# Attention, then a top-8 lookup: the masked logits and their extreme in one VectorE instruction

## The chip, the cores and the metric

One core of one Trainium2 chip runs the whole program. The metric is the device time of one execution in microseconds. The kernel before took 624.84 us, the median of 3 runs (624.62 to 629.85).

## The reference, cut to what matters

16 batches of 128 rows by 1024 columns go through a cross attention and then through a feed-forward part with a table of 256 slots. The change touches the second part alone:

```python
query = hidden_states @ Wq.T
rq = query @ Wr.T
rk = aux_keys @ Wr.T
router_scores = einsum(rq, rk) / sqrt(48) + log_rel
top_scores, top_idx = top_k(router_scores, 8)
sel_keys = aux_keys[top_idx]
attn = einsum(query, sel_keys) / sqrt(64) + log_rel[top_idx]
w = softmax(attn)
aux_out = (w @ aux_values[top_idx]) @ Wvd.T @ Wvu.T
out = hidden_states + gate * aux_out
```

For each of the 128 rows of a batch, the 8 best of 256 router scores choose which 8 slots take part in a softmax over other scores, the key products.

## The kernel before, in words

The five engines run programs of their own that are written out by hand and tied together by semaphores. There is no planner: the order of the calls in each engine's block is the order of the work.

**Main part.** The attention and the hidden layer of the feed-forward part take the first 572 us or so. Nothing of it is changed but one weight preparation: `scoreB`, a matrix of 65 used rows by 512 columns. Columns 0 to 255 give router scores, columns 256 to 511 key products, and row 64 (`BOT`) holds `log_rel`, brought by two DMAs from POOL's queue (L1143). ScalarE scales the key half at L978 and the router half at L982, in the second period of the attention.

**Tail.** From L757 (TensorE), L1020 (ScalarE), L1191 (GpSimd) and L1486 (VectorE) on, 16 batches pass through a pipeline. Batch b goes through these steps:

- TensorE: `score` (L617) makes 512 columns in PSUM, router scores and key products side by side.
- VectorE: `top_max` (L1337) finds the best eight, `top_replace` (L1342) writes a copy of the scores in SBUF with those eight replaced by `NEG` = -3e38, `top_mask` (L1347) compares that copy with the scores in PSUM: 1 where nothing was replaced. `top_logits` (L1353) adds NEG times that mask to the key products, `logit_max` (L1358) takes the negated maximum.
- ScalarE: `softmax_exp` (L1001) with the sum of the row, then copies for TensorE.
- TensorE: `w_transpose` (L726), `z_product` (L734), and with VectorE's `z_low` (L1368, the low part of the product) `f_product` (L748, L749).
- For batches 0 to 11 ScalarE scales the result (`f_scale`, L1018), GpSimd adds the hidden state (L1196, both inputs in SBUF) and SP stores it. `output_scale` (L1180) on GpSimd gives the scale of two batches at a time from `weight_reciprocal` (L1364) and the gate. For batches 12 to 15 VectorE does both in `finish` (L1377).

VectorE's order for step i is: `top_replace(i)`, `z_low(i-3)`, `top_mask(i)`, `top_max(i+1)`, `top_logits(i)`, at even i `weight_reciprocal`, `logit_max(i)`. In step 2 the last two `query_copy` (L1300) stand behind `top_replace(2)`; TensorE passes L754 only when they are done. The steps for batches 0 and 1 are part of VectorE's `hidden_step(15)` and `hidden_step(16)`. In steps 2 and 3 the gate is worked out (`gate_argument`, `gate_value`).

TensorE's order for step i is: `score(i+1)`, `z_product(i-2)`, `w_transpose(i-1)`, `f_product(i-3)`.

Of the kernel before, what the change touches and what calls it, by code (L numbers as in the profile page):

```python
# [6 lines left out]
ALU = mybir.AluOpType  # L7
ACT = mybir.ActivationFunctionType
AX = mybir.AxisListType.X
# [24 lines left out]
BOT, RDIM, NSLOT, TOPK, VB = 64, 48, 256, 8, 64  # L34
UH = N // 4
UQ = UH + BOT
NEG = -3.0e38
# [3 lines left out]
def wait(engine, sem, value):  # L41

    if value > 0:
        engine.wait_ge(sem, value)
# [12 lines left out]
def attention_ffn_kernel(nc, x, ctx_rows, ctx_cols, WqT_raw, WkT_raw, Wv_rows, WoT_rows, bo_row, g_col, Wuq_cols,  # L57
# [3 lines left out]
    with ctx:  # L61
        def sb(name, shape, dt=F32, scope=ctx):
            return scope.enter_context(nc.sbuf_tensor(name, shape, dt))

        def sem(name):
            return ctx.enter_context(nc.semaphore(name))
# [11 lines left out]
        scoreB = sb("scoreB", [P, 2 * NSLOT])  # L78
# [93 lines left out]
        replaced = sb("replaced", [P, NSLOT], scope=ffn)  # L172
        outside = sb("outside", [P, NSLOT], scope=ffn)
        logits = sb("logits", [P, 2, NSLOT], scope=ffn)
        nlmax = sb("nlmax", [P, 2], scope=ffn)
        w_sb = sb("w_sb", [P, 2, NSLOT], scope=ffn)
# [38 lines left out]
        def score_psum(b):  # L215

            return k_slot[:, b * HALF:(b + 1) * HALF] if b < 2 else small[b % 2]
# [4 lines left out]
        def queries(b):  # L222

            if b == B:
                return range(B - 2, B)
            return range(2 * (b - EARLY - 1), 2 * (b - EARLY))
# [15 lines left out]
        log_rel_in = sem("log_rel_in")  # L242
# [18 lines left out]
        b1_prod = sem("b1_prod")  # L261
        score_ready = sem("score_ready")
        score_zeros = sem("score_zeros")

        x_stats = sem("x_stats")
        x_mv = sem("x_mv")
# [85 lines left out]
        masked = sem("masked")  # L352
        outside_done = sem("outside_done")
        logits_ready = sem("logits_ready")
# [117 lines left out]
        def _(pe):  # L472
# [113 lines left out]
            def h_transpose(b, k):  # L586
                pe.wait_ge(h_done, b + 1)
                wait(pe, hT_hi_done, b - 1)
                wait(pe, hT_lo_done, b - 1)
                for j in range(J):  # L590
                    last = nc.tensor.transpose(slot[k][:, j * P:(j + 1) * P], hbuf[:, k, j * P:(j + 1) * P],
                                               ident[:, :])
                last.then_inc(h_T, 1)

            def hidden_products(b, k):
                pe.wait_ge(hT_hi_done, b + 1)
                pe.wait_ge(hT_lo_done, b + 1)
                before = b if b < EARLY else b - 1
                wait(pe, units_biased, before)
                wait(pe, rows_copied, before)  # L600
                dst = unit_psum(b)
                for j in range(J):
                    for n, (a, c) in enumerate(((0, 0), (1, 0), (0, 1))):
                        last = nc.tensor.matmul(dst[:, 0:UQ], hT[a][:, k, j, :], WuqT[c][:, j, :],  # L604
                                                start=(j == 0 and n == 0), stop=(j == J - 1 and n == 2))
                last.then_inc(units_prod, 1)
# [12 lines left out]
            def hidden_step(b):  # L619
                if b + 1 < B:  # L620
                    if b == 0:
                        pe.wait_ge(q_sub, 4 * B)
                    h_transpose(b + 1, (b + 1) % 2)
                if b == EARLY + 5:
                    pe.wait_ge(logsum_done, 1)
                    pe.wait_ge(query_done, 2 * (b - EARLY - 1))
                    nc.tensor.matmul(logtotal_psum, ones[:, :], logsum[:, :], start=True, stop=True).then_inc(logtotal, 1)
                if b < B:
                    if b == 0:
                        pe.wait_ge(mt_copied, B)  # L630
                        pe.wait_ge(wuq_hi, 1)
                        pe.wait_ge(wuq_lo, 1)
                    if b == EARLY:
                        pe.wait_ge(x1_done, B)
                    if b < B - 1:
                        hidden_products(b, b % 2)
                if b > EARLY:
                    if b == EARLY + 1:
                        pe.wait_ge(units_biased, EARLY)
                        pe.wait_ge(o_copied, 2 * B)  # L640
                        pe.wait_ge(query_ones, 1)
                    if b == EARLY + 5:
                        pe.wait_ge(normv_step, 1)
                    for n in queries(b):
                        query_transpose(n, n % 2)
                if b == B - 2:
                    pe.wait_ge(log_rel_in, 16 * 2)
                    for n in range(2):
                        score(n)
                if b == B - 1:  # L650
                    hidden_products(b, b % 2)
                    pe.wait_ge(query_done, B - 2)
                    for n in range(2, 4):
                        score(n)
# [83 lines left out]
            def f_product(b, k):  # L738
                pe.wait_ge(z_split, b + 1)
                if b == 0:  # L740
                    pe.wait_ge(logits_ready, 2)
                if b - 2 < B - BY_VECTOR:
                    wait(pe, f_scaled, b - 1)
                else:
                    pe.wait_ge(y_last, b - 2 - (B - BY_VECTOR) + 1)
                for n in range(2):
                    cols = slice(n * HALF, (n + 1) * HALF)
                    nc.tensor.matmul(slot[k][:, cols], zT[:, k, :], WvuT_hi[:, cols], start=True, stop=False)  # L748
                    last = nc.tensor.matmul(slot[k][:, cols], zT[:, k, :], WvuT_lo[:, cols], start=False, stop=True)  # L749
                last.then_inc(f_prod, 1)  # L750
# [17 lines left out]
        def _(act):  # L768
# [150 lines left out]
            for b in range(PERIODS):  # L919
                p, o, e = b - 1, b - 2, b - 3  # L920
                for i in range(4):
# [48 lines left out]
                    if b == 1 and i == 1:  # L970
                        act.wait_ge(vv_prod, NSLOT // P)
                        act.wait_ge(rk_prod, 1)
                        nc.scalar.copy(VV[:, :, :].rearrange("p s (r d) -> p s r d", d=VB),
                                       ob[:, 0:2 * VB].rearrange("p (s d) -> p s d", d=VB).unsqueeze(2).broadcast_to(
                                           [P, NSLOT // P, P // VB, VB])).then_inc(vv_copied, 1)
                        nc.scalar.copy(rkT, ob[0:RDIM, NSLOT:2 * NSLOT]).then_inc(rk_copied, 1)
                        act.wait_ge(score_zeros, 1)
                        nc.scalar.mul(scoreB[0:BOT, NSLOT:2 * NSLOT], keysT,  # L978
                                      float(BOT) ** -0.5).then_inc(score_ready, 1)
                    if b == 1 and i == 3:  # L980
                        act.wait_ge(b1_prod, 1)
                        nc.scalar.mul(scoreB[0:BOT, 0:NSLOT], ob[0:BOT, 0:NSLOT],  # L982
                                      float(RDIM) ** -0.5).then_inc(score_ready, 1)
# [12 lines left out]
                hidden_step(b)  # L996

            def softmax_exp(b, k):
                act.wait_ge(logits_ready, b + 1)
                wait(act, w_T, b - 1)  # L1000
                nc.scalar.activation(w_sb[:, k, :], logits[:, k, :], ACT.Exp, bias=nlmax[:, k:k + 1],  # L1001
                                     accum_out=wsum[:, b, :]).then_inc(w_done, 1)

            def wT_copy(b, k):
# [15 lines left out]
            for i in range(1, B + 2):  # L1020
                if has(i - 1):
                    softmax_exp(i - 1, (i - 1) % 2)
                if i == 1:
# [4 lines left out]
                                         scale=0.5).then_inc(gate_tanh, 1)  # L1028
                if i == 3:
                    act.wait_ge(gate_arg, 1)  # L1030
                    nc.scalar.activation(gb[:, :], ga[:, :], ACT.Tanh, bias=half3[:, 2:3],
                                         scale=half3[:, 1:2]).then_inc(gate_tanh, 1)
# [168 lines left out]
        def _(dve):  # L1201
            V = nc.vector
# [141 lines left out]
            def top_mask(b):  # L1344
                dve.wait_ge(top_step, 2 * b + 2)
                wait(dve, masked, b)
                V.tensor_tensor(outside[:, :], replaced[:, :], score_psum(b)[:, 0:NSLOT],  # L1347
                                ALU.is_equal).then_inc(outside_done, 1)

            def top_logits(b):  # L1350
                dve.wait_ge(outside_done, b + 1)
                wait(dve, w_done, b - 1)
                V.scalar_tensor_tensor(logits[:, b % 2, :], outside[:, :], NEG, score_psum(b)[:, NSLOT:2 * NSLOT],  # L1353
                                       ALU.mult, ALU.add).then_inc(masked, 1)

            def logit_max(b):
                dve.wait_ge(masked, b + 1)
                V.tensor_reduce(nlmax[:, b % 2:b % 2 + 1], logits[:, b % 2, :], AX, ALU.max,  # L1358
                                negate=True).then_inc(logits_ready, 1)

            def weight_reciprocal(b):

# [206 lines left out]
```

## Time and profile before

| | |
|---|---|
| median of 3 runs | 624.84 us |
| the profiled execution | 622.58 us |
| its span | 620.8 us |
| PE busy | 592.5 us, 95% of the span |
| DVE busy | 541.1 us, 87% |
| ACT busy | 418.1 us, 67% |
| POOL busy | 409.7 us, 66% |

Of the profiled execution's 622.58 us, 620.8 are the span that the trace covers; 1.8 us lie around it. PE is TensorE (PEld its weight loads), DVE is VectorE, ACT ScalarE, POOL GpSimd. A share of busy time is a mean over parts with different limits; here the tail, the last 49 us, is the part that counts. Starts are microseconds from the span's beginning. Consecutive VectorE instructions overlap a little in the trace, so what one costs the engine is the step from its start to the next start.

### The profile page before, as it was taken

What the parts mean: (1) busy time and instruction counts of PE and PEld (TensorE: products, weight loads), DVE (VectorE), ACT (ScalarE), POOL (GpSimd) and SP (SyncE); (2) the same over time, 40 slices, a digit from 0 to 9 for tenths busy, and PEclk for the clock granted to TensorE, in tenths of its full rate; (3) what the DMA queues carried; (4) which work ended last, traced back from release to release, by engine and by line L of the source; (5) the groups of instructions that cost most, each with busy time, mean ns of one, the idle gap of its engine ahead of it and who ended that gap; (6) DMA issues with size and microseconds to landing.
All of it is one profiled execution on the core that took longest, in us unless ns stands there. A gap on an engine that the chain in (4) does not pass through costs nothing.

```text
span 620.8 us, 11452 instructions
## 1 busy us (share of the span) xinstructions
PE 592.5 (95%) x3718; PEld 516.5 (83%) x3718; DVE 541.1 (87%) x721; ACT 418.1 (67%) x864; POOL 409.7 (66%) x421
## 2 busy tenths in 40 slices
PE   4999999999999999999999999999989799999896
PEld 3778888888888888888888888888878799998574
DVE  5999999999999999999999999999968544866996
ACT  5566667676777676767676676777666576584783
POOL 4964457787767768687878787767655735430494
PEclk9999999999999999999999999999999899999999
DMA  8849695868687685959595868676563600000156
GB/s 315 223 128 231 189 248 167 216 180 207 188 201 212 171 231 154 243 173 242 162 243 169 219 179 204 197 195 175 134 196 109 180 8 2 2 2 0 59 214 271
DMA packets 63530, 106.11 MB, mean 171 GB/s; under 512 B 11392, under 2 KB 43680, under 8 KB 61168
## 3 DMA queue, kind: packets, MB, share of 16 engines
q1 hardware_dynamic: 52576, 84.32, 46.4%
q10 hardware_dynamic: 10000, 18.62, 13.2%
q0 software_dynamic: 896, 2.45, 1.3%
q8 instruction: 30, 0.49, 0.4%
q14 instruction: 28, 0.23, 0.1%
HBM read 46.62 MB, written 25.17 MB: 116 GB/s over the span
## 4 chain that ended last, share of the span: by engine, by line
PE 83%; DVE 4%; DMA 3%; ACT 3%; issue 3%; POOL 2%; ACTq 1%; DVEq 0%; SPq 0%; POOLq 0%
PE ob L548 18%; PE gm L517 16%; PE gm L604 5%; PE q_slot L475 4%; PE turn L501 4%; PE k_slot L477 4%; PE k_slot L475 4%; PE q_slot L477 4%; PE k_slot L476 4%; PE q_slot L476 4%; PE turn L604 4%; PE gm L526 2%; PE turn L559 2%; DMA Wuq_in<-Wuq_cols 2%; PE turn L734 1%
## 5 line engine op out<-in xcount | busy, mean ns | idle before, releaser
L1067 POOL TENSOR_TENSOR qs_sb<-qs_sb,qrec 128x1024 f32<-128x1024 f32 x64 | 122.0, 1906 | 96.3 <-DVE qrec L1257 96.1
L548 PEld LDWEIGHTS ob<-mt_sb,q_hd 128*128 128x128 f32 x1024 | 124.3, 194 | 8.3 <-ACT q_hd L805 3.0
L548 PE MATMUL ob<-mt_sb,q_hd 128*128 128x128 f32 x1024 | 127.9, 279 | 2.4 <-ACT q_hd L805 2.4
L517 PE MATMUL gm<-ekT,ctxT 128*128 128x256 f32 x512 | 118.2, 379 | 0.0
L517 PEld LDWEIGHTS gm<-ekT,ctxT 128*128 128x128 f32 x512 | 95.9, 190 | 13.6
L800 ACT ACTIVATE qs_sb<-qs_sb 128x1024 f32<-128x1024 f32 x64 | 67.9, 1061 | 47.3 <-DVE qs_sb L1246 45.9
L790 ACT ACTIVATE ek<-k_slot,nkm 128x1024 f32<-128x1024 f32 x62 | 69.1, 1114 | 32.7 <-DVE nkm L1221 32.5
L1221 DVE TENSOR_REDUCE nkm<-k_slot 128x1 f32<-128x1024 f32 x62 | 74.0, 1194 | 13.9 <-PE k_slot L477 13.9
L1253 DVE TENSOR_REDUCE qsum<-qs_sb 128x16 f32<-128x1024 f32 x64 | 77.1, 1205 | 7.6 <-ACT qs_sb L800 6.5
L1246 DVE TENSOR_TENSOR qs_sb<-q_slot,qm 128x1024 f32<-128x1024 f32 x64 | 78.4, 1224 | 2.2
L1228 DVE STREAM_TRANSPOSE kt<-ek 128x1024 f32<-128x1024 f32 x64 | 79.0, 1234 | 1.1 <-DMA ekT<-kt 1.1
L1240 DVE TENSOR_REDUCE qm<-q_slot 128x16 f32<-128x1024 f32 x64 | 76.0, 1187 | 0.5 <-issue 0.5
L475 PE MATMUL k_slot<-ctx_hi,WkT_hi 128*128 128x512 f32 x124 | 54.7, 441 | 9.3 <-DVE ctx_lo L1419 7.1
L475 PE MATMUL q_slot<-WqT_hi,xn_hi 128*128 128x512 f32 x128 | 53.0, 414 | 2.3 <-DVE qs_sb L1246 2.3
L1061 POOL TENSOR_TENSOR xn_lo<-xn,xn_hi 128x1024 fp32r<-128x1024 f32 x16 | 38.3, 2396 | 20.2 <-ACT xn_hi L784 20.2
L477 PE MATMUL q_slot<-WqT_lo,xn_hi 128*128 128x512 f32 x128 | 50.3, 393 | 0.0
L476 PE MATMUL q_slot<-WqT_hi,xn_lo 128*128 128x512 f32 x128 | 50.0, 391 | 0.0
L477 PE MATMUL k_slot<-ctx_lo,WkT_hi 128*128 128x512 f32 x124 | 49.3, 398 | 0.0
L476 PE MATMUL k_slot<-ctx_hi,WkT_lo 128*128 128x512 f32 x124 | 49.1, 396 | 0.0
L796 ACT COPY g_sb<-gm 128x512 f32<-128x512 f32 x16 | 9.4, 587 | 54.6 <-PE gm L517 54.6
L845 ACT ACTIVATE junk<-o_sb 128x128 f32<-128x128 f32 x128 | 37.6, 297 | 4.8 <-issue 4.7
L1266 DVE STREAM_TRANSPOSE qt<-qs_sb 128x1024 f32<-128x1024 f32 x32 | 38.0, 1188 | 0.0
(208 smaller groups left out, 1309.9 us busy)
## 6 DMA issues: line engine op xcount, KB each, us to landing
ekT<-kt SPq DMA_DIRECT2D x488, 64.0 KB, 2.9
q_turned<-qt SPq DMA_DIRECT2D x16, 1024.0 KB, 4.8
q_hd<-q_turned ACTq DMA_DIRECT2D x64, 256.0 KB, 5.7
ctx_in<-ctx_rows SPq DMA_DIRECT2D x16, 512.0 KB, 6.1
x_all<-x SPq DMA_DIRECT2D x16, 512.0 KB, 4.7
ctxT<-ctx_cols SPq DMA_DIRECT2D x16, 512.0 KB, 5.5
out<-q_hd SPq DMA_DIRECT2D x15, 512.0 KB, 2.6
Wuq_in<-Wuq_cols ACTq DMA_DIRECT2D x1, 1280.0 KB, 9.3
```

The source lines that it names most:

```text
L475: nc.tensor.matmul(dst, lhs[0], rhs[0], start=True, stop=False)
L476: nc.tensor.matmul(dst, lhs[1], rhs[0], start=False, stop=False)
L477: return nc.tensor.matmul(dst, lhs[0], rhs[1], start=False, stop=True)
L517: last = nc.tensor.matmul(gm[:, cols], ctxT[:, b % 2, j, :], ekT[:, 2 * half:2 * half + 2, :, j * BLK:(j + 1) * BLK], start=(j == 0), stop ...
L548: last = nc.tensor.matmul(ob[:, (j % 4) * C:(j % 4 + 1) * C], q, mt_sb[:, b % 2, t, :], start=(t == 0), stop=(t == T - 1))
L790: nc.scalar.activation(ek[:, i % 2, :], k_psum(b, i)[:, :], ACT.Exp, bias=nkm[:, i:i + 1], accum_out=ksum[:, b % 2, i:i + 1]).then_inc(k_e ...
L1067: nc.gpsimd.tensor_tensor(e, e, qrec[:, i % 2, :].unsqueeze(2).broadcast_to([P, PAIR, DH]), ALU.mult).then_inc(q_mul, 1)
L1221: V.tensor_reduce(nkm[:, i:i + 1], k_psum(b, i)[:, :], AX, ALU.max, negate=True).then_inc(k_max, 1)
L1228: V.transpose(kt[:, i, :], ek[:, i % 2, :]).then_inc(k_T, 1)
L1240: V.tensor_reduce(qm[:, :], q, AX, ALU.max).then_inc(q_max, 1)
L1246: V.tensor_tensor(qs_sb[:, i % 2, :].rearrange("p (m d) -> p m d", d=DH), q, qm[:, :].unsqueeze(2).broadcast_to([P, PAIR, DH]), ALU.subtra ...
L1253: V.tensor_reduce(qsum[:, :], qs_sb[:, i % 2, :].rearrange("p (m d) -> p m d", d=DH), AX, ALU.add).then_inc(q_sum, 1)
```

## The change

The key products and `log_rel` beside them are negated, so that the extreme wanted is a minimum. `top_mask` no longer compares with PSUM: it looks for the constant NEG in the replaced copy and multiplies by 3e38 in the same instruction, a `tensor_scalar` from SBUF to SBUF. `top_logits` becomes a `tensor_tensor_reduce` that adds and keeps the minimum, and `logit_max` has no instruction left. ScalarE's exponential takes the scale -1. One ScalarE instruction on one row of 256 is added in the attention's second period, behind a wait for the two DMAs of `log_rel`. Who waited for `logits_ready` now waits for `masked`.

```diff
@@ TensorE, hidden_step
                 if b == B - 2:
                     pe.wait_ge(log_rel_in, 16 * 2)
+                    pe.wait_ge(log_turned, 1)
@@ TensorE, f_product
-                    pe.wait_ge(logits_ready, 2)
+                    pe.wait_ge(masked, 2)
@@ ScalarE, second period
                         nc.scalar.mul(scoreB[0:BOT, NSLOT:2 * NSLOT], keysT,
-                                      float(BOT) ** -0.5).then_inc(score_ready, 1)
+                                      -float(BOT) ** -0.5).then_inc(score_ready, 1)
                     if b == 1 and i == 3:
+                        act.wait_ge(log_rel_in, 16 * 2)
+                        nc.scalar.mul(scoreB[BOT:BOT + 1, NSLOT:2 * NSLOT], scoreB[BOT:BOT + 1, NSLOT:2 * NSLOT],
+                                      -1.0).then_inc(log_turned, 1)
@@ ScalarE, softmax_exp
-                act.wait_ge(logits_ready, b + 1)
+                act.wait_ge(masked, b + 1)
                 wait(act, w_T, b - 1)
-                nc.scalar.activation(w_sb[:, k, :], logits[:, k, :], ACT.Exp, bias=nlmax[:, k:k + 1],
+                nc.scalar.activation(w_sb[:, k, :], logits[:, k, :], ACT.Exp, bias=nlmax[:, k:k + 1], scale=-1.0,
@@ VectorE, top_mask
-                V.tensor_tensor(outside[:, :], replaced[:, :], score_psum(b)[:, 0:NSLOT],
-                                ALU.is_equal).then_inc(outside_done, 1)
+                V.tensor_scalar(outside[:, :], replaced[:, :], NEG, -NEG, ALU.not_equal, ALU.mult).then_inc(outside_done, 1)
@@ VectorE, top_logits and logit_max
-                V.scalar_tensor_tensor(logits[:, b % 2, :], outside[:, :], NEG, score_psum(b)[:, NSLOT:2 * NSLOT],
-                                       ALU.mult, ALU.add).then_inc(masked, 1)
+                V.tensor_tensor_reduce(logits[:, b % 2, :], outside[:, :], score_psum(b)[:, NSLOT:2 * NSLOT], 1.0, -NEG,
+                                       ALU.add, ALU.min, nlmax[:, b % 2:b % 2 + 1]).then_inc(masked, 1)
 
             def logit_max(b):
-                dve.wait_ge(masked, b + 1)
-                V.tensor_reduce(nlmax[:, b % 2:b % 2 + 1], logits[:, b % 2, :], AX, ALU.max,
-                                negate=True).then_inc(logits_ready, 1)
+                pass
```

## Rows read from the trace of the kernel before

**Rows 1.** Busy time by engine in 22 us of the tail
```profile
583.00:605.00 22.00, 22.00 (x109) 16.12 (x108) 20.66 (x68) 19.70 (x46) 21.69 (x14) 1.00 0.47 192
```

The columns: the stretch and its length, then busy us of PE, PEld, DVE, ACT and POOL with the number of instructions, the granted clock, the DMA share, GB/s.

**Rows 2.** Chain that ended last, one step of the tail: start, us, what
```profile
586.29 0.86 PE ob L617 x2
...
588.75 0.86 PE gm L617 x2
```

**Rows 3.** PE's timeline: start, us, instruction, idle before and its releaser
```profile
576.02 0.41 PE L726 MATMUL turn<-ident,w_sb 128*128 128x128 f32 x2 [2.25 <-issue]
...
579.43 0.68 PE L734 MATMUL turn<-wT,VV 128*128 128x128 f32 x4 [0.74 <-DVE zT L1368]
...
608.88 0.68 PE L734 MATMUL turn<-wT,VV 128*128 128x128 f32 x4 [0.53 <-DVE zT L1368]
```

**Rows 4.** DVE's timeline at the head of the tail
```profile
573.98 0.41 DVE L1358 TENSOR_REDUCE nlmax<-logits 128x1 f32<-128x256 f32 x1
...
575.18 0.48 DVE L1300 COPY query<-q_slot 128x128 f32<-128x128 f32 x2
```

**Rows 5.** DVE's timeline, one step of the tail
```profile
595.66 0.08 DVE L1342 MATCH_VALUE_LOAD replaced<-top,gm 128x8 f32 x1
...
596.50 0.42 DVE L1347 TENSOR_TENSOR outside<-replaced,gm 128x256 f32<-128x256 f32 x1
597.00 0.43 DVE L1337 MAX8 top<-ob 128x8 f32<-128x256 f32 x1
...
597.78 0.42 DVE L1358 TENSOR_REDUCE nlmax<-logits 128x1 f32<-128x256 f32 x1
598.12 0.08 DVE L1342 MATCH_VALUE_LOAD replaced<-top,ob 128x8 f32 x1
```

**Rows 6.** POOL's timeline, first and last pair of its twelve adds
```profile
583.29 4.72 POOL L1196 TENSOR_TENSOR q_hd<-q_hd,x_all 128x1024 f32<-128x1024 f32 x2
...
607.86 4.73 POOL L1196 TENSOR_TENSOR q_hd<-q_hd,x_all 128x1024 f32<-128x1024 f32 x2
```

**Rows 7.** ACT's timeline: the first scaling of a result
```profile
581.52 1.11 ACT L1018 ACTIVATE q_hd<-k_slot,oscale 128x1024 f32<-128x1024 f32 x1
```

**Rows 8.** One line each: count, duration ns min/median/max, first and last start
```profile
L1457 DVE TENSOR_SCALAR bo_bc<-bo_bc x1: 186/186/186, 19.4 to 19.4; 128x128 f32<-128x128 f32 x1
...
L1116 POOL TENSOR_SCALAR x_all<-x_all,one_rstd,nb x16: 1194/1206/1638, 485.0 to 560.4; 128x1024 f32<-128x1024 f32 x16
```

**Rows 9.** DVE and POOL side by side, timeline from 539 to 544 us
```profile
539.16 1.23 DVE L1479 CAST WvuT_hi<-WvuT_in 128x1024 fp32r<-128x1024 f32 x1
...
539.83 1.64 POOL L1116 TENSOR_SCALAR x_all<-x_all,one_rstd,nb 128x1024 f32<-128x1024 f32 x1
...
541.43 2.38 POOL L1187 TENSOR_TENSOR WvuT_lo<-WvuT_in,WvuT_hi 128x1024 fp32r<-128x1024 f32 x1
541.44 2.65 DVE L1304 TENSOR_TENSOR units<-units,Wu 128x256 f32<-128x256 f32 x1
543.79 1.38 POOL L1116 TENSOR_SCALAR x_all<-x_all,one_rstd,nb 128x1024 f32<-128x1024 f32 x1
```

**Rows 10.** Timeline at the end of the tail, last mask and last exponential
```profile
608.77 0.42 DVE L1347 TENSOR_TENSOR outside<-replaced,ob 128x256 f32<-128x256 f32 x1
...
610.13 0.51 ACT L1001 ACTIVATE w_sb<-logits,nlmax 128x256 f32<-128x256 f32 x1
```

**Rows 11.** The two DMAs of log_rel: duration of the issue, first and last start
```profile
L1143 POOL DMA_DIRECT2D scoreB<-log_rel_row x2: 509/512/516, 27.1 to 27.6; - x2
```

**Rows 12.** Timelines of ACT and POOL where the new ACT instruction goes
```profile
43.81 1.11 ACT L870 ACTIVATE mt_sb<-gm,krec 128x128 f32<-128x128 f32 x4
...
45.77 0.46 POOL L1073 TENSOR_TENSOR mt_sb<-mt_sb,bo_bc 128x128 f32<-128x128 f32 x1
```

**Rows 13.** Groups by line in the tail: busy us, mean ns, idle before
```profile
L1001 ACT ACTIVATION_READ_ACCUMULATOR w_sb<-logits,nlmax 128x1 f32 x16 | 3.0, 187 | 0.0
...
L1001 ACT ACT_TABLE_LOAD x1 | 1.3, 1283 | 0.0
```

More of the change, by code:

```diff
@@ L263, in attention_ffn_kernel @@
         score_zeros = sem("score_zeros")
+        log_turned = sem("log_turned")
         x_stats = sem("x_stats")
```

## The prediction

> **What bounds the kernel now.** All the edits but one lie in the tail, so I read the tail. First the busy time by engine of a stretch in its middle: TensorE works 22.00 of 22.00 us, GpSimd 21.69, VectorE 20.66 [rows 1]. Then the chain of waits, which runs through TensorE there: a score product starts at 586.29 and the next at 588.75, so a step takes 2.46 us, all of it TensorE's own work [rows 2]. Shortening VectorE's part of such a step gives nothing. GpSimd has the same rate by its own length: twelve adds, in pairs from 583.29 to 607.86 for the first and last, which is 24.57 us for ten batches or 2.457 us each [rows 6]. Then TensorE's timeline at both ends, where it does wait: until 576.02 for the two query copies, 0.74 us for the low part of the first z, 0.53 us for one near the end [rows 3]. VectorE sets these. So the reduction that goes away can pay at the head and at the end, not in the eleven steps between.
>
> **The change part by part, if VectorE and GpSimd leave each other alone.** One reduction costs VectorE 0.34 us (597.78 to 598.12) [rows 5]. The mask now takes 0.42 us [rows 5]. The new one is a one-source instruction from SBUF to SBUF; the only such row of size has half the elements and takes 0.186 us [rows 8]. Bounds 0.19 and 0.42; I take 0.25, near the row of its own kind, a gain of 0.17. The fused add-and-minimum shows nowhere. The nearest rows are the mask and the reduction, 0.42 us each over the same 256 elements; above them I put ScalarE's separate reading of a sum, 0.187 us more, and as the far bound its table load, 1.283 us more [rows 13]. No row excludes that it is a little shorter than the two-operand instruction it replaces, so the low bound is 0.40. I take 0.42, since it reads and writes what its neighbours do.
>
> Head: reduction 1 (573.98) stands before the query copies (575.18) [rows 4], and so does mask 1. TensorE starts 0.34 + 0.17 = 0.51 us sooner. Reduction 2 stands before the gate's arithmetic and the first `z_low`, on which TensorE waits at 579.43 [rows 3]: 0.34 more, of which the trace's overlaps leave about 0.3. TensorE is then about 0.8 us ahead and busy without a gap. Reduction 3 and mask 3 also precede the gate and the second reciprocal, so GpSimd's first add comes about 1.05 us sooner, at 582.24.
>
> End: the `z_low` before the wait at 608.88 stands behind reduction 14, so 0.34 us more. The last exponential (610.13) waited for reduction 15 [rows 10]; it moves by the same 0.34, not twice, because the copy in front of it comes from TensorE. Sum: 0.8 + 0.34 = 1.15 us gained.
>
> ScalarE's added instruction costs nothing. Its DMAs were issued by 27.6 us plus 0.5 [rows 11], sixteen microseconds before the place. It pushes `mt_scale` (43.81, 1.11 us) by about 0.4 us, and who waits is GpSimd's bias add, which started at 45.77 [rows 12] behind a longer instruction of its own queue: 44.92 + 0.4 is 45.3, still earlier. If that cover were gone it would cost 0.4 us once. The added waits on TensorE name work finished long before; 0 to 0.05 us each. The other renamed waits come with the same instruction as before or an earlier one.
>
> **The part that speaks against it.** The new mask may need what GpSimd holds. At 541.43 GpSimd starts an add-like instruction with two SBUF inputs, 2.38 us; VectorE starts a two-input one at 541.44 whose row says 2.65 us, where the same 256 elements otherwise take 0.42. It ends 0.28 us after GpSimd's: it stood still for the whole of it. The GpSimd instruction behind it took 1.38 us instead of 1.206 [rows 8, 9]. A one-source instruction from SBUF did it too: during VectorE's cast at 539.16 (1.23 us), GpSimd's took 1.64, 0.43 more than its median. The old mask read one operand from PSUM and ran at 0.42 us while GpSimd was adding [rows 5]. The new one is of the cast's kind, and GpSimd adds almost without a pause from 583 to 612.6.
>
> The Trainium skill says so outright: in "SBUF — State Buffer", section "Who interferes with whom", a VectorE `tensor_scalar` in a mode that uses both its ports and a GpSimd instruction exclude each other, and the later one stands still until the first is done. By that page this mask stands still; by the rate of 0.186 us alone the sum would stay at a gain of 1.15 us. The measured stall of [rows 9] agrees with it for other operations.
>
> What it costs: VectorE's step without waits is 2.46 less the reduction 0.34, less the faster mask 0.17, less the 0.16 us in which `top_max` waited for TensorE (597.00 against 596.50 + 0.34) [rows 5], about 1.8 us. So each mask from batch 5 on arrives during an add and waits some 0.6 us for its end, and VectorE falls into step with GpSimd: one mask between two adds. That alone would be free but for two things. First, an add waits for the mask in its way: by [rows 8, 9] 0.17 us behind 256 two-input elements and 0.43 behind 1024 one-source elements; for 256 one-source ones I take 0.04 to 0.17. Second, the chain from a mask to the next add: mask 0.25, `top_max` 0.35, fused instruction 0.42, exponential 0.51 [rows 10], scaling 1.11 [rows 7] and the signals between come to 2.7 us, against an add of 2.36. With one add a step the two balance at 2.5 to 2.6. So a step costs 2.50 to 2.61 us, I take 2.55.
>
> The last mask, batch 15, comes after eleven adds: 582.24 + 11 x 2.55 = 610.3, against 608.77 [rows 10]. Behind it the reduction is gone, so the last exponential starts 0.74 us later, 611.0 against 610.13: 0.9 us later, and the final additions and stores follow it. With 2.50 it is 0.4 us, with 2.61 1.6 us. Forecast: +0.9 us. The profiled execution becomes 623.5 us (622.58 before; the span 620.8 and 1.8 around it). Its median of runs stood at 624.84, so the time is 624.84 + 0.9, about **625.7 us**, with 625.2 to 626.4 as its own range.
>
> **The rivals.**
> 1. No stall: the mask passes beside GpSimd's adds. For it: no one-source 256-element instruction was seen to stall. Against it: the cast's row. Time 624.84 - 1.15 = 623.7. Chance 0.28.
> 2. The fused instruction does not do what it says: it comes as a sum plus a reading of the extreme, 0.19 us more each [rows 13]. It stands in the chain that sets the step, so about 0.1 us more in each of eleven steps and 0.19 at the end: 625.7 + 1.3 = 627.0. Without the stall the gain shrinks to 0.5 us, 624.3. Chance 0.12.
> 3. Slower by more: the fused instruction has a price at every use, as the table load of 1.283 us has. It decides from about 1.1 us of length, where VectorE's step (1.8 with 0.42) passes 2.46. At 1.70 us the step is 3.1, 0.62 more than now, in fourteen steps: +8.7, and 624.84 + 8.7 = 633.5. For it: nothing in this trace shows its price. Against it: no VectorE instruction here pays more than 0.09 us to prepare another (the value load, 0.08) [rows 5]. Chance 0.07.
>
> **How the numbers follow.** The forecast has 0.48, the three rivals 0.28, 0.12 and 0.07; 0.05 stays for what I do not see, on either side. The range of 8 in 10 takes in rival 1 with its own bound (0.1 lower if the fused instruction is the shortest) and about half a microsecond for the spread of runs (the two closest shown differ by 0.22), hence 623.0; and rival 2 with the wide end of the step, hence 628.0. About 1%, 6.2 us, is what a measurement of this kernel can tell from no change. No case but rival 3 passes that: faster 0.02, same 0.91, slower 0.07.
>
> **What would show each step.** The masks of batches 5 to 15 read 0.6 us or more in the trace and end with an add's end (rival 1: all near 0.25); those of batches 0 to 4 are short. GpSimd's adds go from 2.457 us a batch to about 2.55, their first start from 583.29 to about 582.2. TensorE gets gaps between 583 and 607. VectorE still has one instruction where there were two, near 0.42 us, with no second row beside it (rival 2 wants one). TensorE's first transpose comes 0.5 us sooner than 576.02 against the end of the hidden layer. The forecast is wrong if the masks are short under the adds, if an add often has a gap before it of a microsecond, or if anything before 566 us moves.

## The result and the profile after

The changed kernel took 627.89 us (median of 20 runs), the kernel before 623.33 (20 runs); the ratio is 1.0074, with a 95% interval of 1.0052 to 1.0097. That is slower by about 4.6 us: within the 1% that was called no change, inside the stated range by 0.1 us, and five times the 0.9 us of the forecast. A second series of runs, below, gives 5.6 us, so the loss is no accident of one series. The landing inside the range is partly luck: the range of 623.0 to 628.0 was laid around a kernel before of 624.84 us, the median of its first 3 runs, and over all 20 that median is 623.33. The same 4.6 us on top of 624.84 would have been 629.4.

The tail first. From the start of the last bias addition of the hidden layer to the end of the span it took 620.8 - 571.87 = 48.93 us before, and 54.46 us now: the bias addition is the first row here, the span 627.4 us.

VectorE's timeline of the changed kernel, that row and then two steps of the tail (start, us, instruction, idle before it):

```profile
572.94 0.42 DVE L1298 TENSOR_TENSOR units<-turn,bu 128x256 f32<-128x256 f32 x1 [1.93 <-PE turn L605]
...
590.91 2.01 DVE L1352 TENSOR_SCALAR outside<-replaced 128x256 f32<-128x256 f32 x1
592.95 0.43 DVE L1342 MAX8 top<-gm 128x8 f32<-128x256 f32 x1
593.30 0.40 DVE L1357 CUSTOM_DVE_ANT_0 logits<-outside,ob 128x256 f32<-128x256 f32 x1
593.63 0.08 DVE L1357 DVE_READ_ACCUMULATOR2_ANT nlmax<- 128x1 f32 x1
593.63 0.09 DVE L1347 MATCH_VALUE_LOAD replaced<-top,gm 128x8 f32 x1
...
594.47 0.81 DVE L1352 TENSOR_SCALAR outside<-replaced 128x256 f32<-128x256 f32 x1
...
596.00 0.16 DVE L1366 RECIPROCAL wrec<-wsum 128x2 f32<-128x2 f32 x1
...
596.90 2.01 DVE L1352 TENSOR_SCALAR outside<-replaced 128x256 f32<-128x256 f32 x1
```

These answer to [rows 5]. L1352 is the mask, L1357 the fused instruction, L1366 the reciprocal. The mask reads 2.01 and 0.81 us in turn, where the one before read 0.42. Two steps take 596.90 - 590.91 = 5.99 us, not 4.91. The fused instruction has a second row, the reading of the minimum, but the next instruction starts at the same 593.63: it costs VectorE nothing, and the pair steps on after 0.33 us like its neighbours.

GpSimd's timeline, which answers to [rows 6]:

```profile
584.39 4.75 POOL L1201 TENSOR_TENSOR q_hd<-q_hd,x_all 128x1024 f32<-128x1024 f32 x2
590.24 0.20 POOL L1185 TENSOR_TENSOR oscale<-wrec,gate 128x2 f32<-128x2 f32 x1 [1.10 <-DVE wrec L1366]
590.39 4.74 POOL L1201 TENSOR_TENSOR q_hd<-q_hd,x_all 128x1024 f32<-128x1024 f32 x2
596.24 0.20 POOL L1185 TENSOR_TENSOR oscale<-wrec,gate 128x2 f32<-128x2 f32 x1 [1.10 <-DVE wrec L1366]
...
619.06 0.20 POOL L1185 TENSOR_TENSOR oscale<-wrec,gate 128x2 f32<-128x2 f32 x1
```

Here lies the difference from the forecast. Two adds end at 595.13. GpSimd then stands idle for 1.10 us, five times over, until VectorE's reciprocal (here that of 596.00). That reciprocal comes after `top_max` and the fused instruction, and these come after the short mask (594.47), which ended at 595.28: it had waited for the second of the very adds whose successors now wait for it. The long mask (590.91 to 592.92) waits for the first add of the pair. Each pair of batches goes once round this circle: 4.74 of adds and 1.25 from the last add through mask, maximum, logits, reciprocal and scale.

The waits of the stretch 584 to 619 us say the same (engine, line, for whom: us in total, times, longest):

```profile
POOL oscale L1185 <- DVE wrec L1366: 8.0, 6, 2.5
ACT w_sb L1006 <- DVE nlmax L1357: 7.1, 6, 1.3
...
PE ob L618 <- DVE nlmax L1357: 4.0, 5, 0.9
```

None of these stood above 2.1 us before. TensorE, full in [rows 1], now waits for VectorE in every second step.

One more line is in the profile after and not in that of before: TensorE's granted clock between 577 and 583 us is 0.72 (the stretch, its length, busy us of PE, PEld, DVE, ACT, POOL, then the clock).

```profile
577.00:583.00 6.00, 5.63 (x20) 4.01 (x21) 3.94 (x20) 3.85 (x13) 0.20 (x1) 0.72 0.00 0
```

This drop is in the profiled execution. It is not in every execution of this kernel; the evidence stands below, with its second series.

### The profile page after: what moved, and what is told of

The parts are those of the page before. It is cut to its first block, busy times and chain, and to the rows that moved or that the text cites. A ratio compares the mean times of both kernels' runs of the same rounds, so it can differ in the third digit from the quotient of the medians.

```text
span 627.4 us, 11453 instructions
## 1 busy us (share of the span) xinstructions
PE 596.0 (95%) x3718; PEld 518.4 (83%) x3718; DVE 546.0 (87%) x721; ACT 418.9 (67%) x865; POOL 409.8 (65%) x421
## 3 DMA queue, kind: packets, MB, share of 16 engines
q0 software_dynamic: 896, 2.45, 1.3%
## 4 chain that ended last, share of the span: by engine, by line
PE 81%; DVE 9%; issue 5%; ACT 3%; DMA 1%; ACTq 1%; POOL 0%; DVEq 0%; SPq 0%; POOLq 0%
PE ob L549 18%; PE gm L518 16%; PE gm L605 5%; PE q_slot L476 5%; PE k_slot L476 4%; PE k_slot L478 4%; PE k_slot L477 4%; PE q_slot L478 4%; PE q_slot L477 4%; PE turn L502 4%; PE turn L605 4%; PE gm L527 2%; PE turn L560 2%; DVE outside L1352 1%; PE q_slot L592 1%
```

## The experiments

The tails below all run from the start of that bias addition to the end of the span, so that what happens before 566 us drops out. Theory A: the mask and GpSimd's adds exclude each other. Theory B: the fused instruction makes the time. Each ratio compares with runs of the kernel before taken beside it, whose medians were 622.13 us for the first four experiments, 622.67 for the next three and 621.70 for the last two. It is not simply the quotient of two medians; for differences of under 1 us the tails, one profile each, say more than the medians, and they have no interval.

**The mask alone, on the kernel before.**

```diff
-                V.tensor_tensor(outside[:, :], replaced[:, :], score_psum(b)[:, 0:NSLOT],
-                                ALU.is_equal).then_inc(outside_done, 1)
+                V.tensor_scalar(outside[:, :], replaced[:, :], NEG, None, ALU.not_equal).then_inc(outside_done, 1)
```

> The kernel before with one edit: the mask is made from the replaced copy alone (not equal to the constant, 0 or 1), as a one-source instruction from SBUF to SBUF. Theory A, the mask and GpSimd's adds exclude each other: masks of batches 5 to 15 alternate near 2.0 and 0.8 us, two steps take 6.0 us instead of 4.91, and the kernel is 5 to 6 us slower than before, since nothing is gained at the head and the end. Theory B, the fused add-and-minimum makes the time: masks near 0.28 us, no change within 1 us.

Measured: 629.37 us, ratio 1.0113 (1.0079 to 1.0147), tail 55.05 us. Two rows of its VectorE and one of its GpSimd:

```profile
588.90 0.38 DVE L1347 TENSOR_SCALAR outside<-replaced 128x256 f32<-128x256 f32 x1
591.27 1.63 DVE L1347 TENSOR_SCALAR outside<-replaced 128x256 f32<-128x256 f32 x1
```
```profile
590.22 0.20 POOL L1180 TENSOR_TENSOR oscale<-wrec,gate 128x2 f32<-128x2 f32 x1 [1.09 <-DVE wrec L1363]
```

One line of the change makes the whole loss and more, 6 us in the tail. (About 1 us of them belongs to TensorE's clock, which reads 0.73 between 577 and 583 us here too; an estimate from the head of the changed kernel, below.) The masks read 1.63 and 0.38 us, not the 2.0 and 0.8 that were expected: the reduction still stands in front of each, so each arrives later and waits less, and the circle is the same: adds start at 590.37 and 596.36, 5.99 us apart.

**The fusion alone, on the changed kernel.**

```diff
-                V.tensor_scalar(outside[:, :], replaced[:, :], NEG, -NEG, ALU.not_equal, ALU.mult).then_inc(outside_done, 1)
+                V.tensor_tensor(outside[:, :], replaced[:, :], score_psum(b)[:, 0:NSLOT],
+                                ALU.is_equal).then_inc(outside_done, 1)
```

> The changed kernel with the old comparison against PSUM as its mask. It leaves out the scaling of the mask (0 or 1 in place of 0 or 3e38), so the softmax is taken over all 256 slots; the instructions and their sizes are those of the change. Theory A: steps of 2.46 us as before, the reduction's share gained at head and end, 0.5 to 1.1 us faster than before. Theory B: slower than before by most of the 4.6 us.

Measured: 621.47 us, ratio 0.9995 (0.9963 to 1.0027), tail 47.97 us, 0.96 shorter than before. Its timelines, VectorE and GpSimd:

```profile
588.21 0.42 DVE L1352 TENSOR_TENSOR outside<-replaced,gm 128x256 f32<-128x256 f32 x1
...
606.79 0.29 DVE L1371 TENSOR_TENSOR zT<-turn,zT 64x128 fp32r<-64x128 f32 x1 [0.47 <-ACT zT L1017]
607.57 0.17 DVE L1367 RECIPROCAL wrec<-wsum 128x2 f32<-128x2 f32 x1 [0.48 <-ACT w_sb L1006]
```
```profile
580.40 4.72 POOL L1201 TENSOR_TENSOR q_hd<-q_hd,x_all 128x1024 f32<-128x1024 f32 x2
...
604.92 4.72 POOL L1201 TENSOR_TENSOR q_hd<-q_hd,x_all 128x1024 f32<-128x1024 f32 x2
```

Ten batches in 24.52 us: the step of before, and theory B falls. The first add comes 10.57 us after the bias addition, against 11.42: 0.85 gained at the head. The end gained next to nothing: VectorE reaches the last low parts sooner and then waits 0.47 and 0.48 us for ScalarE.

**The same mask in another form.** 3e38 is added to the copy, which makes the replaced ones zero.

```diff
+        spare = sb("spare", [P, 1], scope=ffn)
...
-                V.tensor_scalar(outside[:, :], replaced[:, :], NEG, -NEG, ALU.not_equal, ALU.mult).then_inc(outside_done, 1)
+                V.tensor_scalar(outside[:, :], replaced[:, :], -NEG, None, ALU.add, ALU.max,
+                                accum_out=spare[:, :]).then_inc(outside_done, 1)
```

> The changed kernel with the mask as one addition of 3e38 to the replaced copy, in the form that also writes out an accumulator; same operands in SBUF, same 256 elements. If the exclusion hangs on the fast mode of the mask (its 0.28 us for 256 elements) and not on where its operand lies, masks read 0.42 us under the adds, steps are 2.46 us, and the kernel is 0.5 to 1 us faster than before. If any one-source instruction from SBUF is held up, it is 4 to 6 us slower.

Measured: 623.07 us, ratio 0.9993 (0.9964 to 1.0022), tail 48.09 us. VectorE and GpSimd:

```profile
586.29 0.42 DVE L1353 TENSOR_SCALAR_CACHE_REDUCE outside<-replaced 128x256 f32<-128x256 f32 x1
586.63 0.08 DVE L1353 DVE_READ_ACCUMULATOR outside<-replaced 128x1 f32 x1
```
```profile
588.30 4.71 POOL L1202 TENSOR_TENSOR q_hd<-q_hd,x_all 128x1024 f32<-128x1024 f32 x2
```

The same operands in the same places, 0.42 us instead of 0.28, and no wait at all under the adds. So reading from and writing to SBUF alone does not collide; the faster form of the instruction does. "SBUF — State Buffer" of the Trainium skill makes exactly this exception, for the `tensor_scalar` that also writes out its accumulator ("Who interferes with whom"); the trace agrees: every mask reads 0.41 or 0.42 us, beside an add or not. One thing is left open: the operator changed too, from a comparison to an addition, and an addition without the accumulator was not run.

**The reciprocal ahead of the mask.**

```diff
+                if i % 2 == 0 and 6 <= i < B:
+                    weight_reciprocal(i - 2)
                 if i < B:
                     top_mask(i)
...
-                if i % 2 == 0 and i <= B:
+                if i % 2 == 0 and i <= B and not 6 <= i < B:
                     weight_reciprocal(i - 2)
```

> The changed kernel with the reciprocal of steps 6 to 14 moved ahead of that step's mask; nothing else. Theory A1: two steps take 6.0 us because GpSimd, after two adds, waits for a reciprocal that stands behind a mask that waited for the second add. Then GpSimd's 1.10 us of idle in each of five pairs goes, two steps take 5.0 to 5.2 us, and the kernel is 4 us or so faster than the changed one, 0 to 1 us slower than before. Theory A2: the step is held by the chain from a mask over exponential and scaling to the next add; then two steps stay near 6 us and the time stays with the changed kernel's, 4.6 us above before.

Measured: 621.60 us, ratio 1.0007 (0.9971 to 1.0042), tail 48.60 us, 5.9 less than the changed kernel's, of which the clock accounts for 1.0 (below). VectorE and GpSimd:

```profile
569.50 0.42 DVE L1298 TENSOR_TENSOR units<-turn,bu 128x256 f32<-128x256 f32 x1 [1.93 <-PE turn L605]
...
586.40 1.11 DVE L1352 TENSOR_SCALAR outside<-replaced 128x256 f32<-128x256 f32 x1
...
589.14 0.78 DVE L1352 TENSOR_SCALAR outside<-replaced 128x256 f32<-128x256 f32 x1
```
```profile
579.95 4.74 POOL L1201 TENSOR_TENSOR q_hd<-q_hd,x_all 128x1024 f32<-128x1024 f32 x2
584.64 0.25 POOL L1185 TENSOR_TENSOR oscale<-wrec,gate 128x2 f32<-128x2 f32 x1
584.98 4.79 POOL L1201 TENSOR_TENSOR q_hd<-q_hd,x_all 128x1024 f32<-128x1024 f32 x2
...
605.13 4.81 POOL L1201 TENSOR_TENSOR q_hd<-q_hd,x_all 128x1024 f32<-128x1024 f32 x2
```

The circle is open: no scale waits any more. The masks still wait (1.11 and 0.78 us against 0.29 free), yet a pair costs 4.79 + 0.25 and the step is (605.13 - 579.95) / 10 = 2.518 us, 0.06 above the step of before. This is the step that the forecast had named for the changed kernel (2.50 to 2.61); it needed this order. The head holds the very instructions of the changed kernel's, and here TensorE's clock stays at 1.00, in this stretch and in the one from 570 to 577 us:

```profile
577.00:583.00 6.00, 5.88 (x29) 4.06 (x27) 5.40 (x18) 4.88 (x12) 3.40 (x4) 1.00 0.01 1
```

The first add comes 10.45 us after the bias addition, against 11.42 before and 11.45 in the changed kernel. The kernel with short adds, the next experiment, has the same head too, a clock of 1.00 and 10.46 us. So the edit's gain at the head is 0.97 us, and in the profiled execution of the changed kernel the drop of the clock took back 1.00.

**Short adds.** The changed kernel with GpSimd adding 64 of the 1024 columns; the rest of the residual is left out.

```diff
-                nc.gpsimd.tensor_tensor(y_out[:, b % YB, :], y_out[:, b % YB, :], X[:, b, :],
+                nc.gpsimd.tensor_tensor(y_out[:, b % YB, 0:64], y_out[:, b % YB, 0:64], X[:, b, 0:64],
```

> The changed kernel with GpSimd's twelve adds on 64 of their 1024 columns; the rest of the hidden state is left out of the output of batches 0 to 11. If the adds are what holds the masks, every mask reads 0.28 us or little more, steps are TensorE's 2.46 us again and the kernel is 0.5 to 1.2 us faster than before. If anything else in the change stretches the steps, they stay near 3 us and it is slower than before by 4 us or more.

Measured: 619.88 us, ratio 0.9962 (0.9926 to 0.9999), tail 46.94 us. VectorE and GpSimd:

```profile
588.43 0.29 DVE L1352 TENSOR_SCALAR outside<-replaced 128x256 f32<-128x256 f32 x1
```
```profile
590.42 0.32 POOL L1201 TENSOR_TENSOR q_hd<-q_hd,x_all 128x64 f32<-128x64 f32 x1
...
605.12 0.32 POOL L1201 TENSOR_TENSOR q_hd<-q_hd,x_all 128x64 f32<-128x64 f32 x1
```

With the long adds gone every mask reads 0.28 to 0.29 us, and six steps take 14.70, 2.45 each, which is TensorE's own rate of [rows 2]. The tail falls by 7.5 us against the changed kernel, 1.0 of them the clock's, and is 2.0 us shorter than before where 0.5 to 1.2 were expected; where the rest comes from stays open. The masks are long because of GpSimd's long adds: with them gone, nothing else in the change stretches a mask or a step.

**No mask at all.** The copy already tells by its constant which entries were taken out; with the key products negated, adding it to them needs no mask. One instruction fewer, and the minimum is a separate one again.

```diff
-                V.tensor_scalar(outside[:, :], replaced[:, :], NEG, -NEG, ALU.not_equal, ALU.mult).then_inc(outside_done, 1)
...
-                V.tensor_tensor_reduce(logits[:, b % 2, :], outside[:, :], score_psum(b)[:, NSLOT:2 * NSLOT], 1.0, -NEG,
-                                       ALU.add, ALU.min, nlmax[:, b % 2:b % 2 + 1]).then_inc(masked, 1)
+                V.scalar_tensor_tensor(logits[:, b % 2, :], replaced[:, :], -NEG, score_psum(b)[:, NSLOT:2 * NSLOT],
+                                       ALU.add, ALU.add).then_inc(masked, 1)
...
+                V.tensor_reduce(nlmax[:, b % 2:b % 2 + 1], logits[:, b % 2, :], AX, ALU.min).then_inc(logits_ready, 1)
```

> No mask instruction: 3e38 is added to the replaced copy and the negated key products to that in one two-operand instruction (one operand in SBUF, one in PSUM), and a minimum follows. As many VectorE instructions as the changed kernel has, none of which takes what GpSimd needs. Steps of 2.46 us; the head and the end gain as an instruction less per batch gives them, 0.8 to 1.3 us faster than before. If the gain of one instruction less is hidden everywhere, 0.

Measured: 622.17 us, ratio 0.9985 (0.9952 to 1.0018), tail 48.52 us. GpSimd's only wait between the pairs, and TensorE's first transpose:

```profile
602.31 0.19 POOL L1185 TENSOR_TENSOR oscale<-wrec,gate 128x2 f32<-128x2 f32 x1 [0.15 <-DVE wrec L1365]
```
```profile
575.33 0.41 PE L728 MATMUL turn<-ident,w_sb 128*128 128x128 f32 x2 [1.65 <-ACT w_sb L1006]
```

No VectorE instruction waits for GpSimd, and ten batches of adds take 24.74 us (582.65 to 607.39), nearly the 24.57 of before. The row names the exponential, but that had ended at 574.48; what ended last before the transpose was the pair of query copies, at 575.12. The head takes 575.33 - 571.78 = 3.55 us instead of 4.15, and of the 0.60 gained the tail keeps 0.41. That is less than the 0.8 to 1.3 us expected, and less than the intervals can tell from nothing.

**No mask, and the query copies earlier.** In [rows 3] TensorE waits until 576.02 for two copies; here they stand behind `top_logits(1)`, before `unit_weights`.

```diff
                     top_logits(1)
+                    for n in queries(B):
+                        query_copy(n, n % 2)
...
-                if i == 2:
-                    for n in queries(B):
-                        query_copy(n, n % 2)
```

> The same, with the last two query copies moved up behind the logits of batch 1, so that TensorE's way into the tail does not wait for them. TensorE then starts its first transpose when the first exponential is done, about 1 us sooner against the end of the hidden layer: 1.5 to 2.3 us faster than before. If ScalarE's table load and order decide there instead, the same as the kernel without this move.

Measured: 621.41 us, ratio 0.9988 (0.9953 to 1.0024), tail 48.04 us.

```profile
573.79 0.41 PE L728 MATMUL turn<-ident,w_sb 128*128 128x128 f32 x2 [1.04 <-ACT w_sb L1006]
```
```profile
571.75 1.28 ACT L1006 ACT_TABLE_LOAD   x1
573.04 0.51 ACT L1006 ACTIVATE w_sb<-logits,nlmax 128x256 f32<-128x256 f32 x1
```

The first transpose now comes 2.93 us after the bias addition, 0.62 less than without the move, and the tail keeps 0.48 of it. The copies stood in the way. Behind them TensorE waits for the first exponential (573.04), and that starts as ScalarE's table load of 1.28 us ends; VectorE's extreme for that batch had been there since 569.04. This is the limit that the expectation named as its other case: the gain of 1.5 to 2.3 us did not come, 0.89 us of tail did.

**The changed kernel again,** unchanged, beside these.

> The changed kernel once more. Two things are asked. Whether the pairs of masks (near 2.0 and 0.8 us) and GpSimd's 1.10 us of idle in every pair stand in a second execution: expected, the same within 0.1 us. And whether TensorE's granted clock of 0.5 for some 4 us near 578 us belongs to the change: if it does it is there again; if it is an accident of an execution, the head of the tail is 1 us shorter here. Time: 4 to 5.5 us above before.

Measured: 627.32 us, 5.6 above before where 4 to 5.5 were expected, ratio 1.0090 (1.0057 to 1.0123), tail 54.44 us. VectorE, GpSimd, and the stretch with the clock:

```profile
590.32 2.01 DVE L1352 TENSOR_SCALAR outside<-replaced 128x256 f32<-128x256 f32 x1
...
593.88 0.82 DVE L1352 TENSOR_SCALAR outside<-replaced 128x256 f32<-128x256 f32 x1
```
```profile
577.00:583.00 6.00, 6.00 (x25) 4.25 (x25) 4.04 (x19) 3.81 (x12) 0.19 (x1) 0.72 0.00 0
```

The circle is there to 0.02 us, and the drop of the clock is there again. But both profiled executions had a mean clock of 0.990. Of the 25 executions of this kernel, five have a mean of 0.998 or more. The drop alone, 6 us at 0.72, takes 1.7 us or 0.0027 of the mean, so it was not in these five. They took 624.67 to 626.27 us, median 625.48; the 14 runs of the kernel before with 0.998 or more have a median of 620.45. So near the full clock the change costs 5.0 us: the loss does not hang on the drop.

**The accumulator form, and the copies earlier.** What the runs point to as the best: the mask in the accumulator form, the fused instruction and the move.

```diff
-                V.tensor_scalar(outside[:, :], replaced[:, :], NEG, -NEG, ALU.not_equal, ALU.mult).then_inc(outside_done, 1)
+                V.tensor_scalar(outside[:, :], replaced[:, :], -NEG, None, ALU.add, ALU.max,
+                                accum_out=spare[:, :]).then_inc(outside_done, 1)
...
                     top_logits(1)
+                    for n in queries(B):
+                        query_copy(n, n % 2)
...
-                if i == 2:
-                    for n in queries(B):
-                        query_copy(n, n % 2)
```

> The mask in the form with an accumulator, which passed beside GpSimd's adds, and the last two query copies moved up behind the logits of batch 1. From the two parts' tails (0.84 us and 0.48 us shorter): 1.0 to 1.5 us faster than before. If the gains of both lie in the same wait, 0.8.

Measured: 621.74 us over 12 runs, ratio 0.9998 (0.9970 to 1.0025), tail 47.58 us, 1.35 shorter than before and the shortest with nothing left out. VectorE's mask in it:

```profile
585.87 0.42 DVE L1353 TENSOR_SCALAR_CACHE_REDUCE outside<-replaced 128x256 f32<-128x256 f32 x1
```

By its runs it is not shown to be faster than the kernel before; no full version is.

**What spreads the runs.** The runs of one kernel lie up to 10 us apart and follow TensorE's mean granted clock. Of the kernel before, 40 runs at a clock of 0.995 or more have a median of 621.3 us, 17 runs at 0.990 or less one of 626.1. A line fitted through 71 runs of before (those taken beside the experiments) and the runs of all the others, with one slope, gives 4.6 us for 0.01 of clock. With the clock taken out in this way, the differences from the kernel before are, with two standard errors: changed kernel +5.0 ± 0.5 us and in its second series +4.4 ± 0.9, mask alone +6.4 ± 1.0, fusion alone -1.0 ± 0.7, accumulator form -0.9 ± 0.7, reciprocal first +0.4 ± 0.7, short adds -2.1 ± 0.7, no mask +0.1 ± 0.6 (with the move -0.2 ± 0.6), accumulator form with the move -1.1 ± 0.6. The signs agree with the tails, except for the reciprocal first and no mask, whose differences are nothing within their errors. It is a fit made afterwards, so it supports a gain of about 1 us for three versions, one of which leaves work out, and does not show it.

## Why the prediction was right in its range and wrong in its size

The changed kernel's tail is 5.53 us longer than the one before, each in one profiled execution. It divides so: head -0.97 (the head of the kernel with the reciprocal first), clock +1.00 (11.45 against 10.45 us from bias addition to first add, same instructions), the stretch from the first add to the last `output_scale` +5.42 (34.67 against 29.25), the rest +0.08. GpSimd's five waits of 1.10 us make up the +5.42. Without the clock's share the tail is 4.5 us longer, near what the runs near the full clock say.

- **The range** was met partly by luck, as said with the result: as a difference, 4.6 us lies outside the 3.2 us that the range left above 624.84. The prediction had named the sign by which it would be wrong, "if an add often has a gap before it of a microsecond", and that sign came: the gap of 1.10 us stands before each pair of adds from the second on (before the small scaling that precedes it).
- **The exclusion** held: masks 5 to 15 wait for GpSimd's adds and end just after one, those before are short. The short adds remove the waits, and so does the accumulator form. The rule of the Trainium skill that was weighed in the prediction ("SBUF — State Buffer", "Who interferes with whom") gave the right sign.
- **The failed step** is "one mask between two adds ... With one add a step the two balance at 2.5 to 2.6". It followed the chain from a mask to the next add through exponential and scaling, and left out `output_scale` (L1180), which stands on GpSimd between each pair of adds and wants VectorE's reciprocal. That reciprocal stands behind a mask that waits for the last add of the pair. So two adds, the wait for them and what follows on VectorE run one after the other, 5.99 us a pair, or 3.0 a step. I had asked what waits for a mask, not what VectorE holds behind it. With the reciprocal in front, and nothing else moved, the measured step is 2.518, inside the 2.50 to 2.61 of the forecast: the estimate fits the kernel without this circle, and the changed kernel has it.
- **Price of the mask:** 0.28 to 0.29 us where nothing is in its way, 0.25 taken. **How much it delays an add:** 0.06 us per step in the kernel with the reciprocal first, the lower part of 0.04 to 0.17.
- **The fused instruction:** 0.40 to 0.42 us, 0.42 taken. Rival 2's second row is there, 0.08 us, and hidden by the next instruction, so it costs nothing; rival 3 is refuted by the fusion alone, whose step is that of before.
- **Head:** 1.05 us forecast for GpSimd's first add; 0.97 with the whole change, 0.85 with the fusion alone. TensorE's first transpose came 0.60 us sooner against the bias addition (576.49 - 572.94 against 576.02 - 571.87), 0.51 forecast. Forecast and measurement agree, but the profiled executions of the changed kernel lost it again to the clock, which no step of the prediction had.
- **End:** 0.34 forecast. The fusion alone has 0.96 in all, 0.85 of it from the head; VectorE then waits for ScalarE (0.47 and 0.48 us), so some 0.1 is left. I moved the last exponential by VectorE's time and did not ask what ScalarE did before it: in the kernel before, its copy of 609.82 (0.37 us) ends as late as the reduction that I took for the limit (609.68, 0.42 us).
- **ScalarE's added instruction** costs nothing that the trace shows, but by less than was worked out. It pushed `mt_scale` by 0.7 us, not 0.4 (from 1.36 us behind the start of the exponential before it, at 42.45, to 2.07 behind the one at 42.65). GpSimd's bias addition still started behind the longer instruction of its own queue (44.10, 1.91 us), 0.1 us after `mt_scale` had ended:

```profile
43.87 0.41 ACT L984 ACTIVATE scoreB<-scoreB 1x256 f32<-1x256 f32 x1
...
44.72 1.14 ACT L872 ACTIVATE mt_sb<-gm,krec 128x128 f32<-128x128 f32 x4
```
```profile
45.97 0.46 POOL L1078 TENSOR_TENSOR mt_sb<-mt_sb,bo_bc 128x128 f32<-128x128 f32 x1
```

- **Rival 1,** no stall, is what the accumulator form does: its tail is 0.84 us shorter, against 1.15 worked out.
- **No change within 1%** came true because 5.5 us of a tail and 4.6 us in the medians is still less than 6.2.

## What to carry to other kernels

When an instruction may be held by another engine's, list what stands behind it in its own queue and who waits for that, down to the instructions of 0.2 us: if one of them releases the holder's next piece of work, the delay is paid in full at every turn. Such a circle can be opened by order (the small releasing instruction in front of the one that is held) or by form (an instruction that is slower alone and does not wait). And an engine's step that is read off its own queue is only a bound: draw the edges in both directions before adding up.

## What the runs showed of the hardware that I had not expected

- An instruction on the same operands took 0.28 us as a plain comparison and 0.42 as an addition that also writes an accumulator, and only the first was held by GpSimd, for as long as 1.7 us (2.01 against 0.29). The slower form made the tail 6.4 us shorter (48.09 against 54.46), 1.0 of them the clock's.
- The delay was uneven here: VectorE's mask waited up to 1.7 us for what was left of an add of 2.36, while a pair of GpSimd's adds grew from 4.72 to 4.80 us beside the short masks.
- TensorE's granted clock explains most of the spread of this kernel's runs. In the kernel before, one stretch ahead of the tail's last microseconds stands at a lower clock, the one that begins after TensorE had waited 2.56 us until 484.40 and 1.10 us until 486.59; the kernel with the reciprocal first waited 1.83 and 1.10 us in the same place and shows no drop. The columns are as in the stretches above, the first for the kernel before, the second for the reciprocal first:

```profile
485.00:490.00 5.00, 3.90 (x21) 3.66 (x20) 1.85 (x3) 3.32 (x10) 4.05 (x4) 0.66 0.42 138
```
```profile
485.00:490.00 5.00, 4.22 (x34) 4.22 (x35) 1.15 (x3) 4.29 (x12) 4.03 (x4) 1.00 0.44 125
```

  In the first TensorE runs 21 groups where the second runs 34: part of it at 1.2 instead of 2.4 GHz. But the changed kernel waited 1.82 and 1.10 us there and did drop (its clock is 0.57 in the same stretch), so the waits alone don't decide it.
- The second drop, at 577 to 583 us, was seen in both profiles of the changed kernel and in that of the mask alone, and in no other. Those three also had the longest drop at 485 to 495 us (a clock of 0.66 or 0.67 over these 10 us, against 0.83 to 1.00 in the other profiles). The kernel with the reciprocal first has the same head and neither. As the five runs near the full clock show, neither drop is in every execution of the changed kernel; whether its waits make them more frequent is not shown. What ties the two drops together was not found, and stays open.
